# Attention scores that open with one 512-column bf16 shift product, ahead of the maxima pair

## What is computed

```python
qh = proj(q, Wq, bq)
kh = proj(k, Wk, bk)
vh = proj(v, Wv, bv)
scores = jnp.einsum('bhqd,bhkd->bhqk', qh, kh) / np.sqrt(D_K)
attn = jax.nn.softmax(scores, axis=-1)
out = jnp.einsum('bhqk,bhkd->bhqd', attn, vh)
...
x = x + _L0_xattn_ref(_layernorm(x, axis=-1), ctx_1024, ctx_1024, ...)
x = x + _L0_attn_ref(_layernorm(x, axis=-1), ...)
x = x + _L0_ffn_ref(_layernorm(x, axis=-1), ...)
```

## Time and profile before

| | us |
|---|---|
| median of 3 runs | 684.64 |
| lowest and highest | 683.98, 685.73 |
| the profiled execution, its own time | 684.26 |
| its span in the trace | 682.4 |
| PE busy | 655.0 (96%) |
| DVE busy | 473.3 (69%) |
| ACT busy | 326.9 (48%) |
| POOL busy | 296.1 (43%) |

### The profile page before, as it was taken

One profiled execution on the slowest core, in us unless ns is written; L12 is line 12 of the kernel. 1 busy time (PEld: TensorE's weight loads), 2 busy tenths in 40 slices (PEclk: granted clock), 3 DMA queues, 4 the chain that ended last, 5 costly groups with the idle time before them and its releaser, 6 DMA issues.

```text
span 682.4 us, 16188 instructions
## 1 busy us (share of the span) xinstructions
PE 655.0 (96%) x6618; PEld 538.7 (79%) x6626; DVE 473.3 (69%) x870; ACT 326.9 (48%) x533; POOL 296.1 (43%) x386
## 2 busy tenths in 40 slices
PE   7989999999999989999999999979999999999996
PEld 4778878878867867877887787656788999999996
DVE  4887757667657688584977857479778666666653
ACT  4355655554454554455446453446555444444431
POOL 1137797896676688675668766400000000000000
PEclk9999999999999999999999999999999999999999
DMA  5311110100010010011001000062003203320000
GB/s 164 144 49 51 28 48 26 49 26 26 26 35 16 26 50 25 26 34 41 9 20 48 1 2 1 2 248 88 37 1 124 103 22 124 123 109 14 0 0 31
DMA packets 12853, 34.12 MB, mean 50 GB/s; under 512 B 1515, under 2 KB 9972, under 8 KB 10612
## 3 DMA queue, kind: packets, MB, share of 16 engines
q1 hardware_dynamic: 12756, 33.19, 14.6%
q0 software_dynamic: 32, 0.01, 0.0%
HBM read 32.67 MB, written 0.52 MB: 49 GB/s over the span
## 4 chain that ended last, share of the span: by engine, by line
PE 81%; DVE 9%; issue 5%; ACT 2%; POOL 2%; DMA 0%; POOLq 0%; DVEq 0%; ACTq 0%
PE bank L1154 45%; PE bank L1340 13%; PE bank L1163 9%; PE bank L1224 5%; POOL prob_sum L481 2%; PE bank L1264 2%; PE bank L1273 2%; DVE prob_sum L481 1%; DVE ctx_lo L465 1%; DVE maxes L877 1%; ACT probs L719 1%; ACT k_hi L615 1%; PE bank L1248 1%; DVE k_lo L858 1%; PE bank L1370 1%
## 5 line engine op out<-in xcount | busy, mean ns | idle before, releaser
L481 POOL TENSOR_TENSOR prob_sum<-probs,prob_sum 128x256 f32<-128x256 f32 x336 | 266.3, 824 | 80.6 <-ACT probs L719 76.3
L719 ACT ACTIVATE probs<-bank 128x1024 f32<-128x1024 f32 (+1 forms) x104 | 106.6, 1025 | 122.9 <-PE bank L1340 107.9
L877 DVE TENSOR_REDUCE maxes<-bank 128x1 f32<-128x400 f32 (+1 forms) x256 | 131.3, 566 | 21.6 <-PE bank L1224 19.7
L701 ACT ACTIVATE h_raw<-bank,b_sb 128x512 f32<-128x512 f32 (+2 forms) x72 | 46.1, 641 | 106.5 <-PE bank L1154 106.3
L858 DVE SCALAR_TENSOR_TENSOR k_lo<-bank,bias_sb,k_hi 128x400 fp32r<-128x400 f32 (+2 forms) x64 | 40.4, 632 | 50.3 <-ACT k_hi L615 50.2
L1154 PE MATMUL bank<-w_hi,h_hi 128*128 128x256 f32 x256 | 72.7, 284 | 0.0
L1154 PE MATMUL bank<-w_hi,h_lo 128*128 128x256 f32 x256 | 72.2, 282 | 0.0
L1340 PE MATMUL bank<-qbd_hi,k_hi 64*128 64x256 f32 (+1 forms) x416 | 71.8, 339 | 0.3 <-issue 0.3
L1154 PE MATMUL bank<-w_lo,h_hi 128*128 128x256 f32 x256 | 72.1, 281 | 0.0
L1163 PE MATMUL bank<-probs,v_sb 128*32 128x128 f32 (+1 forms) x1664 | 67.0, 279 | 2.5 <-DVE masked L812 2.0
L1154 PE MATMUL bank<-wv_hi,ctx_hi 128*128 128x256 f32 (+1 forms) x208 | 65.2, 314 | 2.2 <-DVE maxes L877 1.9
(11 more groups left out here) (157 smaller groups left out, 1427.0 us busy)
## 6 DMA issues: line engine op xcount, KB each, us to landing
raw<-in_w SPq DMA_DIRECT2D x16, 1024.0 KB, 6.8
ctx_raw<-in_ctx_t SPq DMA_DIRECT2D x16, 400.0 KB, 3.7
ctx_raw<-in_ctx_t SPq DMA_DIRECT2D x8, 402.0 KB, 3.6
ctx_raw<-in_ctx_t SPq DMA_DIRECT2D x8, 399.0 KB, 3.6
w_sb<-in_w_t SPq DMA_DIRECT2D x1, 1280.0 KB
w_raw<-in_w_t SPq DMA_DIRECT2D x2, 256.0 KB, 4.6
result<-x_all SPq DMA_DIRECT2D x1, 512.0 KB, 3.0
x_all<-in_x SPq DMA_DIRECT2D x1, 384.0 KB, 4.2
```

Source lines behind the costliest of these rows:

```text
L481: ins = engine.tensor_tensor(prob_sum[0:ROWS[k], cols], probs[0:ROWS[k], s % 2, cols], acc[0:ROWS[k]], ALU.add)
L701: nc.scalar.activation(h_raw[:, c % 2, 0:width], bank[:, at, 0:width], ACT.Gelu, bias=b1_sb[:, bass.ds(e, 1), c:c + 1].rearrange("p a b -> ...
L719: nc.scalar.activation(probs[0:ROWS[k], s % 2, :].rearrange("p (g n) -> p g n", g=G), bank[0:ROWS[k], score_bank(b, k):score_bank(b, k) + ...
L877: nc.vector.tensor_reduce(maxes[:, g * PAIRS + j, c:c + 1], src[:, 0:width], AX.X, ALU.max).then_inc(read_dve, 1)
```

## The change

`scores` is cut in two. `shift_scores` makes the waits that `scores` made and then the bf16 product, once per row tile with 512 columns (both head groups) in place of twice with 256, with the flag that starts the sum. `scores` keeps the three fp32r parts, which add to it. In a step that has an M pair ahead, `shift_scores` now stands ahead of that pair and the fp32r parts behind it; at k = 12 both stay behind the X units. `scores_done` is now signalled by an fp32r product (the low keys of group 1) and no longer by the bf16 one. The number of columns, M units, evictions and DMAs is the same. Per step there are 14 score products and weight loads instead of 16.

```diff
-            def scores(units, b, bi, k):
+            def shift_scores(units, b, bi, k):
...
                     units.wait_shift(pe, read_act, bi)
                     units.wait_keys(pe, read_dve, bi)
+                for r in range(ROW_TILES):
+                    at = slice(RT * r, RT * r + RT)
+                    nc.tensor.matmul(bank[0:rows, score_bank(b, k) + r, :], ones_bf[at, 0:rows],
+                                     shift_rows[at, bi, :, r * RH * Q:(r + 1) * RH * Q], start=True, stop=False,
+                                     skip_group_check=True)
+
+            def scores(b, bi, k):
+
+                rows = ROWS[k]
                 keys = slice(k * P, k * P + rows)
                 for g in range(G):
-                    for part in range(4):
+                    for part in range(3):
                         for r in range(ROW_TILES):
                             at = slice(RT * r, RT * r + RT)
-                            if part < 3:
-                                stays = (k_hi, k_hi, k_lo)[part][bi][at, g, keys]
-                                moves = (qbd_hi, qbd_lo, qbd_hi)[part][at, bi, g].rearrange("p h q -> p (h q)")
-                            else:
-                                stays = ones_bf[at, 0:rows]
-                                moves = shift_rows[at, bi, g, r * RH * Q:(r + 1) * RH * Q]
+                            stays = (k_hi, k_hi, k_lo)[part][bi][at, g, keys]
+                            moves = (qbd_hi, qbd_lo, qbd_hi)[part][at, bi, g].rearrange("p h q -> p (h q)")
                             ins = nc.tensor.matmul(bank[0:rows, score_bank(b, k) + r, g * RH * Q:(g + 1) * RH * Q], stays, moves,
-                                                   start=(part == 0), stop=(part == 3))
+                                                   start=False, stop=(part == 2), skip_group_check=True)
                 ins.then_inc(scores_done, 1)
...
                     if k == 2:
                         weigh(b, bi, 0)
+                    if k != SHIFT_AT:
+                        shift_scores(units, b, bi, k)
                     for n, kind, u in units.at[s][:units.ahead[s]]:
                         unit(units, n, kind, u, t - 1, b + 1, (bi + 1) % 2)
-                    scores(units, b, bi, k)
+                    if k == SHIFT_AT:
+                        shift_scores(units, b, bi, k)
+                    scores(b, bi, k)
```

## The result

The changed kernel took 676.46 us (median of 4 runs, 674.82 to 678.35), the kernel before 685.18 (median of 4, 683.98 to 688.52), a ratio of 0.9858 [0.9824, 0.9892]: 8.7 us faster, where 12.2 had been forecast. That lies in the wide range of the prediction (669 to 679), but above the forecast's own range (670 to 675.5). The profiled execution took 677.73, its span is 675.9.

The account below looks back on a forecast made before the run. PE bounds the kernel (busy 96% of the span). Gross 14.0 us less 2.6 lost in waits plus 0.8 won back gives 12.2: 672.1, or 672.4 for the median; own range 670 to 675.5, 8-in-10 range 669 to 679.

Parts of the forecast that it names:

- Rival B: Score steps: the new bf16 pair hides no weight load, only 2 us won, 682.5 us; chance 6%.
- Rival C: 512-column bf16 pair: its row tiles run one behind the other, 0.21 more per step, 694 us; chance 3%.
- rival D: M steps: less room than 0.52, the exponential's wait shows; break-even at 0.19 us in each of 63 steps; chance 2%.
- the step that had the least room: b = 1, k = 9: 0.52 us left between the exponential's end and the bf16 pair's start; moved wait costed at nothing.
- gross: All score steps: 63 M steps save 0.145, 33 with nothing ahead 0.135, eight k = 12 0.05; 14.0 us.
- batch ends b = 0/1 and 1/2: Gains of k = 10, 11, 12 and 0 vanish in PE's wait for the keys; loss 0.2 and 0.3 us.
- b = 3 and 5: Gains of k = 9, 10, 11 lost in the shift wait, which grows as M comes 0.23 later; 0.65 us each.
- b = 6 and b = 7: PE's waits for DVE's chain hide four steps in b = 7 (0.5 us); two like waits cost batch 6 0.3.
- k = 3, won back: k = 3 of b = 0, 1, 2, 4: bf16 pair runs during the M pair's wait for keys; gains 4 x 0.2 = 0.8 us.
- the size of one step's gain: M step: 0.23 + 0.17 + 0.585 (five distances of 0.117) + 0.21 = 1.195 against 1.34, 0.145 us saved.
- The 0.05 of k = 12: Step k = 12: about 1.02 us after against 1.07 before, 0.05 us saved, eight times.
- rival A: Helpers POOL and DVE fall behind in more batches than named and take 6 us of the gain, 678.5 us; chance 16%.

Follow-up runs that it names:

- Experiment 2: Changed kernel with the one 512-column bf16 product put behind the M pair again: 682.75 us, ratio 0.9961.
- again: The changed kernel rerun with no edit, traced in an execution at full clock: median 675.49 us, ratio 0.9865; executions at clock 1.0 took 674.86 to 674.92.
- experiment 6: Kernel before, with three of four pieces of POOL's sums for k = 8 to 12 left out (result incomplete): 684.35 us, ratio 0.9971.
- experiment 7: Changed kernel, with three of four pieces of POOL's sums for k = 8 to 12 left out (result incomplete): 671.89 us, ratio 0.9801.
- experiment 9: Changed kernel with filler products in two last-batch waits, DVE instead of POOL making the sum of k = 9 in batches 0 and 1: 673.32 us, ratio 0.9812.
- experiment 8: Changed kernel with filler products in two last-batch waits, M pair first again at k = 9 of b = 3 and 5: 674.43 us, ratio 0.9831.
- experiment 3: Changed kernel with the bf16 products still first, but as two pairs of 256 columns: 676.65 us, ratio 0.9879.
- experiment 4: Changed kernel with bf16 filler products (8 and 11) in two PE waits of the last batch: 674.53 us, ratio 0.9836.
- experiment 5: Kernel before, with the same bf16 filler products (8 and 11) in the same two last-batch waits: 684.42 us, ratio 0.997.
- experiment 10: Changed kernel with filler products in two last-batch waits, DVE making the sum of k = 9 in batches 0, 1, 3 and 5: 672.89 us, ratio 0.9807.

## Why the prediction was right in the mechanism and 4 us off in size

**Right.** The mechanism holds: one bare fp32 load becomes a bare bf16 load. The stretches of the new step came out as worked out (in the step shown 0.40 for 0.40, 0.60 for 0.585, 0.21 for 0.21; with nothing ahead 1.02 for 1.025). Experiment 2 shows that 0.10 of the 0.13 in the M steps hangs on the order alone. Rival B (no load hidden, 682.5) is refuted by those distances. The rule of the Trainium skill ("TensorE: Matmul & The Clock Gate", "What overlaps and what doesn't") does not hold here either: behind a bf16 pair fp32 loads to the same row groups stay hidden, as the earlier trace rows had shown. Rival C (row tiles one behind the other) would have made the 0.40 into 0.61. Of rival D (the exponential bare) there are two instances, at 137.27 and 141.69, both where POOL holds ACT; in the step that had the least room, b = 1, k = 9, PE does not wait.

**Wrong in size**, from 12.2 forecast to 9.4 measured at full clock ("again"; the terms are sums of the ledger's steps, rounded):

| term | forecast | measured | difference |
|---|---|---|---|
| gross: 63 steps at 0.129, not 0.145, 33 at 0.134, 8 at 0.033, not 0.05 | 14.0 | 12.8 | -1.2 |
| batch ends b = 0/1 and 1/2 | -0.5 | -1.0 | -0.5 |
| b = 3 and 5 | -1.3 | -1.2 | +0.1 |
| b = 6 and b = 7 | -0.8 | -0.7 | +0.1 |
| k = 3, won back | +0.8 | +0.45 | -0.35 |
| end of b = 7 | 0 | -0.45 | -0.45 |
| start, before the first step | 0 | -0.5 | -0.5 |
| sum | 12.2 | 9.4 | -2.8 |

- The step that failed most is the size of one step's gain. I took a mean distance of 0.117 from three numbers rounded to 0.01, and 0.40 to the first fp32r pair from two rows that are not this step; the medians are 0.594 for the five (not 0.585) and 0.41. Together 0.016 too much, 63 times, is 1.0. The 0.05 of k = 12, eight times, was 0.1 too much.
- At the batch ends I counted what is hidden in M's wait (0.45) but not that POOL, already without a pause, falls behind by what each shorter step takes from it; its backlog grew from 16 to 20 pieces, and ACT's exponential and the denominators came late as well. Experiments 6, 7 and 9 show that this is POOL's doing. That is rival A, in places that I had already named.
- For b = 3 and 5 the sum was right and a reason wrong. The wait grew by 0.28, not by 0.65: the gains of k = 10 and 11 are hidden in it (0.27), k = 9 gains nothing, k = 4 little, and the 0.23 by which the first M pair comes later costs nothing (experiment 8).
- At k = 3 of b = 2 the M pair starts 0.80 behind the start of `weigh` (153.25 - 152.45 before, 150.79 - 149.99 after), with or without the bf16 pair under it. So it still stands for its keys, which the prediction had ruled out, and such a step gains about 0.24, 0.11 more than others, not 0.2 more.
- The end of b = 7 is a term I did not have: rival A again, with DVE as the helper, in a place that I had not named. DVE's steps there are sum and `w_lo`, without a pause, in "again" (timeline of DVE, then of PE):

```profile
459.32 1.22 DVE L481 TENSOR_TENSOR prob_sum<-probs,prob_sum 128x1024 f32<-128x1024 f32 x1
460.46 0.69 DVE L1012 TENSOR_TENSOR w_lo<-raw,w_hi 128x512 fp32r<-128x512 f32 x1
461.06 1.22 DVE L481 TENSOR_TENSOR prob_sum<-probs,prob_sum 65x1024 f32<-65x1024 f32 x1
```

```profile
462.33 0.64 PE L1163 MATMUL bank<-prob_sum,ones_f 128*32 128x128 f32 x16 [1.15 <-DVE prob_sum L481]
```

That is 1.74 us per step, and PE's step there was 1.74 before and is 1.60 now. PE's wait for the last sum grows from 0.71 (below, before) to 1.15: the gains of the last steps are not there.

```profile
471.71 0.64 PE L1163 MATMUL bank<-prob_sum,ones_f 128*32 128x128 f32 x16 [0.71 <-DVE prob_sum L481]
```

- The start differs between executions of one kernel (from 0.4 us later than before to 1.3 earlier in the traces here), with the moment at which the granted clock is first full (9.7 us into the span before, 10.6 in "again", 3.9 in experiment 3, by the traces' clock records). It is scatter, not the change; without it the change is worth 9.9 by this ledger, as by experiments 4 and 5.

So 2.8 us of the miss is the table, and 1.5 the half clock; the forecast of 672.4 had allowed 0.4 for the median, which leaves about the 4.1 between it and 676.46. The steps of the prediction that failed are thus the size of a step's gain, POOL at the batch ends, k = 3 and the end of b = 7. The half clock has another cause: it comes in the kernel before too, and goes in both when the waits are filled (experiments 4 and 5). My forecast spoke for an execution at full clock, which the profiled one of before had been. The traces of one execution could not show it; the scatter of the median could have made me ask.

## What to carry to other kernels

Where TensorE changes the shape of its tile, try a bf16 product first: in these steps what stood there paid its weight load bare (0.11 us for fp32; about 0.02 for bf16, an estimate from these distances), and an fp32 load behind it was hidden. When steps get shorter, look at every engine that already runs without a pause, since it falls behind by what each step gains, and a slow DVE operation beside a long row of POOL operations may be POOL's fault. If executions of one kernel scatter, read the granted clock by windows and see what TensorE did before it fell; some products thrown into the wait took 1.0 us off the median of the changed kernel on one chip (675.49 to 674.53) and 1.9 off that of the kernel before on another (686.32 to 684.42).

## What the runs showed of the hardware

- TensorE's clock fell to the lower level (1.2 GHz) behind waits of 1.99 and 2.94 us in one execution and not in another of the same kernel ("again"). It also fell at waits of 0.54 and 1.15 us close together in experiments 9 and 10, and not at the same two in "again" and experiment 4. A fall cost 1 to 3 us in the traces and in most times; the slowest execution before (691.86, mean clock 0.983) lies 7.6 above the full clock's 684.3. Behind the filled waits of 1.99 and 2.94 (2.67 before) it stayed full in all six profiles that have fillers.
- Three DVE operations of 0.22 us took 0.66 to 0.71 beside POOL's two-input sums and a fourth of the same form 0.23; a copy of 8 columns took 0.65 instead of 0.17.
- One bf16 product of 512 columns in place of two of 256 saved 0.003 us per step (0.3 us in 91 steps, experiment 3 against "again").
